# The vector engine's loop of layer 0 announces its closing branch

## The reference

```python
x = pair_rep normalised over (C, H, W) * ln_w + ln_b
q, k, v = proj(wq), proj(wk), proj(wv)            # 'oc,bcij->boij', 4 heads x 64
g = sigmoid(proj(wg_w) + wg_b)
bias = einsum('hc,bcij->bhij', wb, x)
scores = einsum('bhcij,bhcik->bhijk', q, k) / 8 + bias[:, :, None]
o = g * einsum('bhijk,bhcik->bhcij', softmax(scores), v)
x = x + einsum('oc,bcij->boij', wrep_w, o) + wrep_b
```

## Time and profile before

| | us |
|---|---|
| median of 3 runs | 5077.78 (5075.72 to 5081.89) |
| the profiled execution | 5074.54 |
| its span | 5072.7 |

### The profile page before, as it was taken

One profiled execution on the slowest core, in us unless ns is written; L12 is line 12 of the kernel. 1 busy time (PEld: TensorE's weight loads), 2 busy tenths in 40 slices (PEclk: granted clock), 3 DMA queues, 4 the chain that ended last, 5 costly groups with the idle time before them and its releaser, 6 DMA issues. The chain is left out here.

```text
span 5072.7 us, 150113 instructions
## 1 busy us (share of the span) xinstructions
PE 4726.3 (93%) x44087; PEld 3890.6 (77%) x44087; DVE 4027.1 (79%) x12779; ACT 3552.5 (70%) x11216; POOL 3459.8 (68%) x5926
## 2 busy tenths in 40 slices
PE   4664999999999999999999979999999999999999
PEld 2332878778787787787877857888888888888887
DVE  4445888888888888888888887888888888888887
ACT  2332888888888888888888856666666666666665
POOL 2333888888788888788878845666666666666665
PEclk8776999999999999999999989999999999999999
DMA  8993111111111111111111101111111111111111
GB/s 329 360 359 135 56 54 51 57 50 58 50 58 51 50 58 50 58 50 55 54 50 58 50 26 48 54 50 50 50 50 50 50 53 53 50 50 50 50 50 44
DMA packets 237474, 383.70 MB, mean 76 GB/s; under 512 B 18756, under 2 KB 156616, under 8 KB 224968
## 3 DMA queue, kind: packets, MB, share of 16 engines
q1 hardware_dynamic: 237256, 381.63, 22.5%
HBM read 309.21 MB, written 72.35 MB: 75 GB/s over the span
## 5 line engine op out<-in xcount | busy, mean ns | idle before, releaser
L1300 POOL TENSOR_SCALAR l_probs<-l_probs,l_inv 128x256 f32<-128x256 f32 x2048 | 943.3, 478 | 737.5 <-DVE l_inv L1205 731.9
L543 POOL TENSOR_SCALAR l_probs<-l_probs,l_inv 128x256 f32<-128x256 f32 x2048 | 982.1, 492 | 475.1 <-DVE l_inv L795 475.1
L1124 ACT ACTIVATE l_probs<-bank,l_neg_max 128x256 f32<-128x256 f32 x2048 | 947.4, 481 | 487.2 <-DVE l_neg_max L1199 487.2
L714 ACT ACTIVATE l_probs<-l_probs,l_neg_max 128x256 f32<-128x256 f32 x2048 | 1012.3, 503 | 6.3 <-DVE l_neg_max L787 6.3
L787 DVE CUSTOM_DVE_ANT_0 l_probs<-bank,bias 128x256 f32<-128x256 f32 x2048 | 749.6, 421 | 263.1 <-PE bank L656 187.0
L1199 DVE TENSOR_REDUCE l_neg_max<-bank 128x2 f32<-128x512 f32 x1024 | 646.1, 683 | 93.4 <-PE bank L1033 93.4
L1212 DVE TENSOR_TENSOR l_probs_t<-bank,bias 128x512 f32<-128x512 f32 x1024 | 674.0, 681 | 36.0 <-PE bank L1043 10.4
L656 PE MATMUL bank<-ident,l_probs 128*128 128x128 f32 x4096 | 603.9, 280 | 1.4 <-POOL l_probs L543 1.1
L668 PE MATMUL bank<-l_probs_t,l_v 128*64 128x256 f32 x4096 | 555.1, 392 | 38.9 <-DVE l_probs_t L809 38.3
L656 PEld LDWEIGHTS bank<-ident,l_probs 128*128 128x128 f32 x4096 | 444.7, 141 | 135.5 <-issue 99.0
L1043 PE MATMUL bank<-ident,l_probs 128*128 128x128 f32 x4096 | 531.8, 273 | 3.4 <-DVE l_probs_t L1212 1.7
(11 more groups left out here) (193 smaller groups left out, 14046.6 us busy)
## 6 DMA issues: line engine op xcount, KB each, us to landing
fp_x<-in_x_dram SPq DMA_DIRECT2D x32, 1024.0 KB, 6.9
fp_ln_w<-in_L_conv_ln_w_dram SPq DMA_DIRECT2D x32, 1024.0 KB, 8.9
fp_ln_b<-in_L_conv_ln_b_dram SPq DMA_DIRECT2D x32, 1024.0 KB, 10.5
fp_pair<-in_L_conv_pair_repr_dram SPq DMA_DIRECT2D x32, 1024.0 KB, 12.8
l_x<-in_x_dram SPq DMA_DIRECT2D x128, 256.0 KB, 2.9
l_ln_w<-in_L_conv_ln_w_dram SPq DMA_DIRECT2D x128, 256.0 KB, 3.4
l_ln_b<-in_L_conv_ln_b_dram SPq DMA_DIRECT2D x128, 256.0 KB, 3.6
x<-l_y SPq DMA_DIRECT2D x128, 256.0 KB, 2.0
```

The lines of the kernel that those rows point to most:

```text
L543: last = nc.gpsimd.tensor_scalar(probs[:, h, c], probs[:, h, c], inv[:, h, c:c + 1], 1.0, ALU.mult, ALU.mult)
L714: last = nc.scalar.activation(probs[:, h, c], probs[:, h, c], ACT.Exp, bias=neg_max[:, h, c:c + 1], scale=-1.0, accum_out=total[:, h, c:c ...
L1124: last = nc.scalar.activation(probs[:, h, c], b_s[h % 4][:, c * W:(c + 1) * W], ACT.Exp, bias=neg_max[:, h, c:c + 1], accum_out=total[:, h ...
L1300: last = nc.gpsimd.tensor_scalar(probs[:, h, c], probs[:, h, c], inv[:, h, c:c + 1], 1.0, ALU.mult, ALU.mult)
```

## The change

```diff
-def loop_ends_peeled(engine, count, body):
+def loop_ends_peeled(engine, count, body, hinted=None):
+
 
     body(0, True, False)
-    with engine.Fori(1, count - 1) as t:
+    with hinted.Fori(1, count - 1, engines=[engine.engine], hint_back_edge=True) if hinted else engine.Fori(1, count - 1) as t:
         body(t, False, False)
     body(count - 1, False, True)
...
-def over_rows(engine, total, unroll, row, ahead=3, behind=1):
+def over_rows(engine, total, unroll, row, ahead=3, behind=1, hinted=None):
...
-    loop_ends_peeled(engine, total // unroll, body)
+    loop_ends_peeled(engine, total // unroll, body, hinted)
...
-        def rows(engine, row):
-            over_rows(engine, W, UNROLL, row, ahead=AHEAD, behind=1)
+        def rows(engine, row, hinted=None):
+            over_rows(engine, W, UNROLL, row, ahead=AHEAD, behind=1, hinted=hinted)
...
-            rows(dve, row)
+            rows(dve, row, hinted=nc)
```

## The result

The changed kernel takes 5019.31 us (median of 4 runs, 5018.31 to 5020.96), the kernel before beside it 5079.55 us (4 runs). The ratio is 0.9882, with a 95% interval of 0.9865 to 0.9900. The forecast was 5020 us.

What follows compares the result with a forecast made beforehand. PE was taken as the bound, except for DVE's instruction-fetch stall once per layer 0 iteration. 5074.5 - 59.0 + 1 = 5016.5, plus 3.3 for the median, gave 5020 us; range 5011 to 5048, about 80%.

Steps and rivals of the forecast that it cites:

- The bound and the price of an edge: Layer 0 is PE-bound except at each loop jump: 1.85 us times 29, 53.7 us, or 59.0 with clock drops.
- The slack: At layer 0's loop jump, up to 0.93 us of DVE lateness costs nothing, since the row waits for PE.
- The clock: PE's clock falls behind three of layer 0's 29 edges, about 1.7 us each, 5.1 us, gone without the stall.
- The jump and the new instruction: DVE's announced jump and the added instruction at layer 0's loop head were each taken to cost zero.
- The exit: Behind layer 0's last iteration, the code behind the loop is late once: 1 us, bounds 0 and 3.5.
- The mechanism: In DVE's layer 0 loop, 2.9 of the jump's 3.2 us is refetching the head, by the body's length.
- Part of the fetch staying: Rival, 7%: layer 0's announced block is requested too late, 0.92 us a jump stay, 27 us, so 5046.
- The code in between being pushed out: Rival, 5%: the early head displaces the middle of layer 0's DVE loop, adding a second stall: 5131 to 5137 us.
- layer 1: Rival, 2%: DVE's layer 1 loop shifts one place across another block; its 29 jumps stall, ending at 5074 to 5104.

Runs made afterwards that it cites:

- The second execution of before: The kernel before, unchanged, profiled a second time: 5081.3 us (one run).
- The kernel at place 64: Kernel before, not announced, DVE's layer 0 body shortened by one wait per inverse step, its first instruction 64 instructions into a piece: 5228.4 us (one run).
- its sister with layer 1 announced: The kernel at place 64 with DVE's loop of layer 1 announced and layer 0 untouched: 5070.6 us (one run).
- The stall by hand: Changed kernel plus unused DVE addition work heading each of 30 layer 0 iterations, three lengths: 5020.6, 5025.7, 5085.1 us; the longest used two additions.
- place 111: Changed kernel with DVE's layer 0 loop starting 111 instructions into a piece; 24 intended empty instructions left no record: 5024.0 us (one run).
- five pieces: Changed kernel with 24 one-element memsets added to DVE's layer 0 body, started 111 into a piece, layer 1's loop at a piece's start: 5030.1 us.

## Why the prediction was right

**The bound and the price of an edge.** Right: 59.0 us for layer 0 from 1.85 us an edge and the clock drops, 58.9 measured. That the forecast of 5020 is met to 1 us is luck in the last digits: the rest of the program came out 4 us longer than in the profiled execution from which I subtracted, and 3.3 us had been added for the median.

**The slack.** 0.93 us was forecast from one stall; 1.04 and 1.05 were measured with stalls of other lengths. DVE's stall is what PE paid for. With a slack of 1.05 us a lateness of 2.78 us would cost 1.73 and it cost 1.85, so any other cost of the fetch is about 0.1 us a jump.

**The clock.** The drops were forecast to go with the stall, and went: no kernel whose jump is cured has one in layer 0. The second execution of before bears out their number, 3 again. But not every such stall has them. The kernel at place 64 has 1 drop in layer 0 (at 1130.8 us), its sister with layer 1 announced none, with the same stall of DVE and slightly shorter pauses of PE: 34.5 and 33.8 us in 29 pieces, where before has 37.4. The stall by hand has none either, with 27.4 us in 29. The numbers 3, 1, 0 and 0 go in the order of the pause, but I varied nothing to test that, so what decides stays open.

**The jump and the new instruction.** Zero was taken for both. The jump takes 0.3 us and the instruction 39 ns, and the slack holds them.

**The exit.** 1 us was taken. In the changed kernel DVE has no wait for "issue" there, so nothing was paid. The way from layer 0's last branch to layer 1's first is 271.7 us before (2938.4 to 3210.1) and 272.6 after (2880.1 to 3152.7), but 270.5 in the second execution of before, and PE's wait for the DMA of `l_x` in it grew from 1.8 to 3.0 us. The mechanism that I named, that the code behind is late once, is real all the same: it shows in seven of the nine kernels with DVE's loop of layer 0 announced (1.7 to 3.8 us of DVE), and where PE felt it most, at place 111, it waited 2.4 us, within the bounds of 0 and 3.5. Why the changed kernel escapes it, while two by-hand kernels whose loop starts at the same place stop for 1.7 and 1.9 us there, stays open.

**The mechanism** was right in its effect and wrong in its reason. I wrote that 2.9 us pass "until the code of the loop's head is there again", which holds, and took it from the length of the body alone. It was the length with the placement, and the one piece fetched behind the loop: 358 instructions stall or don't by 64 places. I also wrote that nothing in the trace tells when the fetch begins; the packets of the instruction queue do. The Trainium skill, "Runtime: NRT & Kernel Launch", section "Instruction fetch mechanics", has 512 instructions held, which agrees with four pieces of 128. Its blocks of 256 do not agree with DVE's packets of 8 KB, and its "purely sequential" fetch not with the head that came 0.9 us ahead of an announced branch. The measurements decide.

**The rivals.** Part of the fetch staying (5046) did not happen; its mechanism shows with five pieces, and there costs 0.47 us a period, 14 us, not 27. The code in between being pushed out did not happen, since the whole body is held. The one that I mis-sized is layer 1. I priced a bad placement at 1.85 to 2.9 us a jump, 54 to 84 us, after layer 0's, and the runs show 67.93 - 62.43 = 5.5 us, 160 us: PE waits 3.1 us in each iteration, and the clock falls behind 27 of the 29 jumps, which I had left out. At that price the case would have ended near 5180, far outside my range. I gave it 2%, for "one place in some 260". With pieces of 128 a loop of 264 lies across four of them at 7 places of 128 (121 to 127), and one place further makes it so in 1 case of 128: an estimate from the lengths measured here. The changed kernel moved that loop by one place and it went well.

## What to carry to other kernels

Look at the queue that carries instructions within a loop: if it has packets in every iteration, the loop loses its head, and the next question is whether the engine that everybody waits for sees the jump. A loop that almost fits can be cured by an announcement, or by thirty instructions less together with the right place. The announcement is the simpler (39 ns an iteration), and with it the same body took the same 2228.6 to 2228.7 us at three places. It can cost a stop of some 2 to 4 us once, behind the loop, so it is for loops that lose their head and not for all. Any edit of an engine's program moves the loops behind it, so compare these packets in all loops before a difference is put down to the edit.

## What the runs showed of the hardware

- DVE's instruction packets are 8 KB, and the stops at the exit fit pieces of 128 instructions. Without announcement a body of three such pieces stays (358 instructions from a piece's start) and one of four does not; with it four stay (390, 414), and five are fetched in each round.
- An unannounced jump whose head is gone took 3.2 us in layer 0 and 2.8 us in layer 1, a jump with the head there 0.3 us, and an announced one whose head was fetched 0.9 us ahead 0.9 us.
- Behind the last branch of an announced loop DVE stopped once for 1.7 to 3.8 us in seven kernels of nine, where the next piece begins, and PE once for 2.35 us in the kernel where its own loop was announced.
- The granted clock fell to half for 3.4 us, about 7 us behind a jump, in 3, 3, 1 and 0 of 29 jumps in four executions with PE pauses of 1.3, 1.3, 1.2 and 1.2 us (means), each followed by one of 0.4 us. With pauses of 3.1 us it fell in 27 of 29, mostly for 6.8 us.
